# Three raw block buffers, output projections from the third head step, an earlier low half and an earlier input load

## The reference, cut to what matters

```
xn  = layernorm(x)                                  # 2048 tokens x 512
q, k, v, u = split(xn @ W_qkvu.T); q, k = silu(q), silu(k)
o   = causal linear attention with per-head decay, 16 heads of 32, a running state
A   = (u * o * rsqrt(mean(o*o) + 1e-6)) @ W_out.T
s   = xn @ w_router; idx = top 256 tokens by s      # "selected"
h   = rms_norm(xn[idx]); 16 query heads, 8 key/value heads of 128, rotary, causal softmax
x1  = xn[idx] + attention(h) @ wo
mlp = silu(rms_norm(x1) @ w_gate) * (rms_norm(x1) @ w_up) @ w_down   # inner width 2048
F   = xn, with the selected rows gated between xn[idx] and x1 + mlp
out = x + A + F
```

## Time and profile before

| | us |
|---|---|
| median of 3 runs | 521.44 (521.37 to 521.46) |
| profiled execution | 522.22 |
| its span in the profile | 520.5 |
| PE busy | 490.6 |
| DVE, ACT, POOL busy | 304.1, 230.3, 216.2 |

### The profile page before, as it was taken

The page is one execution under the profiler, slowest core; times in us unless marked ns, Lnnn a source line. Parts: engine busy times, 40 slices in busy tenths (PEclk is TensorE's granted clock), DMA queues, the critical chain, the costliest instruction groups (busy, mean ns, idle before and its releaser), DMA issues.

```text
span 520.5 us, 10501 instructions
## 1 busy us (share of the span) xinstructions
PE 490.6 (94%) x4143; PEld 448.1 (86%) x4143; DVE 304.1 (58%) x615; ACT 230.3 (44%) x404; POOL 216.2 (42%) x191
## 2 busy tenths in 40 slices
PE   6986999999999999999998988999999989999984
PEld 6976999899998998989988877898888778999773
DVE  5958468664479888662646565987675426230231
ACT  7820241212245766512232426465758765453330
POOL 3012235323023311325066666644426332778882
PEclk9997999999999999999999997999999999999999
DMA  7914242133300110002412543565556622455423
GB/s 253 372 44 128 74 122 70 55 103 102 122 23 21 45 42 21 21 21 83 161 42 83 184 161 137 169 212 172 203 173 219 215 82 82 141 163 162 161 82 40
DMA packets 32880, 62.05 MB, mean 119 GB/s; under 512 B 3440, under 2 KB 3456, under 8 KB 32704
## 3 DMA queue, kind: packets, MB, share of 16 engines
q1 hardware_dynamic: 32288, 60.08, 35.0%
q0 software_dynamic: 544, 1.31, 1.4%
HBM read 48.27 MB, written 13.12 MB: 118 GB/s over the span
## 4 chain that ended last, share of the span: by engine, by line
PE 74%; POOL 5%; issue 4%; ACT 3%; DVE 3%; DMA 3%; DVEq 0%; ACTq 0%; POOLq 0%
PE bank L1211 24%; PE bank L1165 8%; PE bank L1202 8%; PE bank L1167 8%; PE bank L1166 7%; POOL wlo L1103 4%; PE bank L1230 3%; PE bank L1274 3%; PE bank L1264 3%; PE bank L1258 3%; ACT whi L514 2%; PE bank L1421 1%; PE bank L1251 1%; DMA raw<-in_w_gate 1%; PE bank L1181 1%
## 5 line engine op out<-in xcount | busy, mean ns | idle before, releaser
L1103 POOL TENSOR_TENSOR wlo<-raw,whi 128x512 fp32r<-128x512 f32 x96 | 127.9, 1364 | 92.0 <-ACT whi L514 92.0
L1088 POOL TENSOR_TENSOR state<-kv_new,state_dec 128x512 f32<-128x512 f32 x15 | 21.8, 1452 | 126.6 <-DVE kv_new L790 126.6
L1165 PE MATMUL bank<-HTh,whi 128*128 128x256 f32 x224 | 66.2, 296 | 1.9 <-ACT whi L514 1.2
L1167 PE MATMUL bank<-HTh,wlo 128*128 128x256 f32 x224 | 64.3, 287 | 0.0
L1166 PE MATMUL bank<-HTl,whi 128*128 128x256 f32 x224 | 64.3, 287 | 0.0
L779 DVE TENSOR_TENSOR A<-bank,DEC 128x512 f32<-128x512 f32 x64 | 39.7, 682 | 31.0 <-PE bank L1230 29.9
L514 ACT ACTIVATE whi<-raw 128x2048 fp32r<-128x2048 f32 x24 | 45.8, 1910 | 22.9 <-DMA raw<-in_w_down 14.4
L1165 PEld LDWEIGHTS bank<-HTh,whi 128*128 128x128 f32 x224 | 44.0, 197 | 3.3 <-issue 2.7
L1211 PE MATMUL bank<-xTh,WKh 128*128 128x256 f32 x128 | 38.7, 302 | 6.5 <-DVE xTl L712 6.5
L1166 PEld LDWEIGHTS bank<-HTl,whi 128*128 128x128 f32 x224 | 44.0, 196 | 0.3
L1167 PEld LDWEIGHTS bank<-HTh,wlo 128*128 128x128 f32 x224 | 43.9, 196 | 0.0
(11 more groups left out here) (237 smaller groups left out, 1344.4 us busy)
## 6 DMA issues: line engine op xcount, KB each, us to landing
X<-in_x SPq DMA_DIRECT2D x16, 256.0 KB, 4.2
xn_all<-XN SPq DMA_DIRECT2D x16, 256.0 KB, 2.8
uo_all<-uo SPq DMA_DIRECT2D x16, 256.0 KB, 2.6
raw<-in_wq SPq DMA_DIRECT2D x4, 1024.0 KB, 5.3
UR<-uo_all SPq DMA_DIRECT2D x16, 256.0 KB, 4.6
XR<-in_x SPq DMA_DIRECT2D x16, 256.0 KB, 2.9
out<-XR SPq DMA_DIRECT2D x16, 256.0 KB, 2.0
raw<-in_wo SPq DMA_DIRECT2D x4, 1024.0 KB, 5.8
```

The costliest lines, as they stand in the source:

```text
L1088: Q.tensor_tensor(state[:], kv_new[:], state_dec[:], ALU.add).then_inc(state_ok, 1)
L1103: ins = Q.tensor_tensor(low[:, k, :], raw[b % 2][:, k, :], high[:, k, :].bitcast(f32), ALU.subtract)
L1165: T.matmul(dst, lh, rh, start=first, stop=False)
L1167: return T.matmul(dst, ll, rh, start=False, stop=last)
```

## The change

There are six edits. A third raw buffer is added, in room of the first stage that is free once the tokens are chosen; block 0 waits for idx_ps instead of proj_ps, and block b from 3 on for `block_lo(b-3)`. SP issues most block loads one block earlier. The high and low halves of the blocks stand earlier in ACT's and POOL's lists of slots 13 to 15; on POOL both low halves of slots 13 and 14 stand ahead of the state's sum. The output projections start in step 2 (`OUT_AT = 2`), with all their loads, halves, sums and stores. The last `rms` and `mean_square` stand in step 0, behind TensorE's unit and ACT's exponentials. In slot -1 `xt_low(3)` is first in DVE's list behind the mask, and SP issues `load_x(M + 2)` ahead of `store_xn(M)`.

```diff
-        raw = [at(f"raw{i}", 8 * i, [P, 4, DM]) for i in range(2)]
+        raw = [at(f"raw{i}", kb, [P, 4, DM]) for i, kb in enumerate((124, 0, 8))]
...
-        PT_AT, PV_AT, WO_AT = 2, 3, 4
+        PT_AT, PV_AT, WO_AT, OUT_AT = 2, 3, 4, 2
...
-            bank_jobs += [("out", h)] if h < late_outs[0] else []
+            bank_jobs += [("out", h - OUT_AT)] if 0 <= h - OUT_AT < late_outs[0] else []
...
                 k = order[b]
-                if b < 2:
+                if b == 0:
+                    sp.wait_ge(idx_ps, 1)
+                elif b < 3:
                     sp.wait_ge(proj_ps, NPROJ * (G - 1) + 2)
                 else:
-                    sp.wait_ge(fw_lo, b - 1)
-                sp.dma_start(raw[b % 2][:], source[k[0]](int(k[1]))).then_inc(raw_in[b % 2], 16)
+                    sp.wait_ge(fw_lo, b - 2)
+                sp.dma_start(raw[b % 3][:], source[k[0]](int(k[1]))).then_inc(raw_in[b % 3], 16)
...
                 for M in ln_tiles(N):
-                    store_xn(M)
                     if M + 2 < N_TILES:
                         load_x(M + 2)
+                    store_xn(M)
...
                 if N >= 1:
                     mean_square(N - 1)
+                if N == N_TILES - 3:
+                    block_hi(1)
                 if N == N_TILES - 2:
-                    block_hi(2)
-                if N == N_TILES - 1:
-                    block_hi(4)
-                    split_uo(0)
+                    block_hi(3)
...
-            mean_square(N_TILES - 1)
-            block_hi(5)
+                if N == N_TILES - 3:
+                    block_hi(2)
+                if N == N_TILES - 2:
+                    block_hi(4)
...
                     ins.then_inc(exp_ok, 1)
+                if h == 0:
+                    mean_square(N_TILES - 1)
...
                     mask(N)
+                if N == -1:
+                    xt_low(N + XT_AHEAD)
...
                 if N >= N_TILES - 3:
                     block_lo(2 * (N - (N_TILES - 3)))
+                    block_lo(2 * (N - (N_TILES - 3)) + 1)
                 if 0 <= N < N_TILES - 1:
                     new_state(N)
                 if -1 <= N < N_TILES - 1:
                     state_decayed(N + 1)
-                if N >= N_TILES - 3:
-                    block_lo(2 * (N - (N_TILES - 3)) + 1)
...
-            rms(N_TILES - 1)
...
                     unit(unit_of_step[h])
+                if h == 0:
+                    rms(N_TILES - 1)
...
-                if h < late_outs[0]:
-                    project_out(h)
+                if 0 <= h - OUT_AT < late_outs[0]:
+                    project_out(h - OUT_AT)
```

More of the change, by code:

```diff
@@ L72, in build @@
                     for part, homes in (("h", (112, 158, 96, 104)), ("l", (116, 162, 100, 108))))
-        VA = [at(f"VA{i}", kb, [P, NS, DM]) for i, kb in enumerate((92, 124))]
+        VA = [at(f"VA{i}", kb, [P, NS, DM]) for i, kb in enumerate((92, 120))]
         X = at("X", 120, [P, NX, DM])
@@ L416, in _ @@
                     load_x_again(1)
-                    load_block(4)
                 if N == N_TILES - 1:
                     load_block(5)
+                    load_block(6)
             store_uo(N_TILES - 1)
-            load_block(6)
-            load_uo(2)
+            load_block(7)
             for h in range(STEPS):
-                if h + 3 < N_TILES:
-                    load_uo(h + 3)
-                if h < late_outs[0]:
-                    store(h)
-                if h + 2 < N_TILES:
-                    load_x_again(h + 2)
+                if 2 <= h + 1 < N_TILES:
+                    load_uo(h + 1)
+                if 0 <= h - OUT_AT < late_outs[0]:
+                    store(h - OUT_AT)
+                if 2 <= h < N_TILES:
+                    load_x_again(h)
                 if h in load_at:
                     load_block(block_of[load_at[h]])
-            for b in range(block_of["U1"] + 1, len(order)):
+            for b in range(block_of["D0"] + 1, len(order)):
                 load_block(b)
-                if b == block_of["U1"] + 1:
+                if b == block_of["D0"] + 1:
                     for N in late_outs:
@@ L511, in block_hi @@
             def block_hi(b):
-                act.wait_ge(raw_in[b % 2], 16 * (b // 2 + 1))
+                act.wait_ge(raw_in[b % 3], 16 * (b // 3 + 1))
                 act.wait_ge(*last_use(b))
-                S.activation(halves(b)[0][:], raw[b % 2][:], ACT.Copy).then_inc(fw_hi, 1)
+                S.activation(halves(b)[0][:], raw[b % 3][:], ACT.Copy).then_inc(fw_hi, 1)
             def hidden_high(n):
@@ L936, in _ @@
                 in_position(N, 1)
-                if N == N_TILES - 1:
-                    uo_low(0)
-                if CH < N + XT_AHEAD < N_TILES:
+                if CH + 1 < N + XT_AHEAD < N_TILES:
                     xt_low(N + XT_AHEAD)
@@ L970, in _ @@
                     ins.then_inc(sm_ok, 1)
-                if h < late_outs[1]:
-                    uo_low(h + 1)
+                if 0 <= n + 1 < late_outs[2]:
+                    uo_low(n + 1)
                 if h < FH:
@@ L979, in _ @@
                     stage(unit_of_step[h])
-                if h < late_outs[0]:
-                    final(h)
+                if 0 <= n < late_outs[0]:
+                    final(n)
                 if 0 <= g < FH:
@@ L1102, in block_lo @@
                 for k in range(4):
-                    ins = Q.tensor_tensor(low[:, k, :], raw[b % 2][:, k, :], high[:, k, :].bitcast(f32), ALU.subtract)
+                    ins = Q.tensor_tensor(low[:, k, :], raw[b % 3][:, k, :], high[:, k, :].bitcast(f32), ALU.subtract)
                 ins.then_inc(fw_lo, 1)
```

31 lines of the change are left out of this document (15 added, 16 removed).

## The result

The changed kernel takes 508.71 us (median of four runs, 507.23 to 509.07) against 521.45 for the kernel before, which had runs of 521.37 to 523.16 beside it. The ratio is 0.9733, with a 95% interval of 0.9704 to 0.9761. The forecast was 505.6 with a range of 503.3 to 511. The profiled execution takes 508.65 with a span of 506.9, where before had 522.22 and 520.5: 13.6 us of span are gone, and 15.8 had been forecast. By the medians it is 12.7, mainly since the profiled execution of the kernel before was 0.8 above its median. So 508.71 lies inside the wide range, but above the 504 to 507.5 that went with the forecast itself.

A forecast was written before the change was run, and what follows sets the result against it. TensorE was taken as the bound, at full clock nearly everywhere, the change being worth the stops it removes: 6.1 + 4.6 + 1.6 + 3.5 = 15.8 us, from 521.44 to 505.6 us, range 503.3 to 511.

The forecast's parts named there:

- (a): Rival: the lower clock comes back behind waits in steps 2 and 3 or slot 0, costing about 3.1 us: 508.7; chance 0.18.
- (c): Rival: the early gain is halved, DVE's norms of tiles 5 to 8 slow down, keys come at 48: 508.7; chance 0.10.
- part 2: Slots 13 to 15 and steps 0 to 3: earlier block halves, later rms and moved projections gain 4.6 us, bounds 1.5 and 6.5.
- Part 1: Slot -1: xt_low(3) first and the input load ahead of the store gain 6.1 us, bounds 4.5 and 8.1.
- Part 2 up to the end of unit 8: Slots 13 to 15: stops of 1.53, 2.54 and 2.40 go; 7.6 us won, some given back later.
- Part 2 behind unit 8: Steps 0 to 3: rotations delay the first projection 1.2 us and unit 11 2.4 us, leaving 4.6 us won.
- The price of 2.9 by that rule for part 2: Steps before unit 11: if POOL slows both uo_low to 1.72 us each, the gain is 2.9 instead of 4.6.
- Part 3: Steps 13 and 14: projections moved there fill the gaps and gain 1.6 us, bounds 1.0 and 2.0.
- Part 4: The end: loads waiting for the low half three back remove stops of 1.20, 0.42 and 1.45; gain 3.5, bounds 1.5 and 3.7.
- (b): Rival: POOL and ACT, not the raw buffers, set the end's pace, which then gives 0.5: 508.6; chance 0.08.
- (d): Rival: in the middle fw_hi of blocks 3 and 5 waits for late units, stops stay, only rms moves: about 508; chance 0.08.
- (e): Rival: block loads hold up SP's one queue in steps 2 to 17, 16 us and more lost: 522 to 526; chance 0.02.

The follow-up runs named there:

- e1: Changed kernel with only xt_low(3) put back behind the norms of tiles 5 and 6, early input load kept; 510.37 us, ratio 0.9787.
- e2: Changed kernel with only SP's order put back, store_xn(M) ahead of load_x(M+2); 512.27 us, ratio 0.9811.
- e4: Changed kernel with only TensorE's last rms put back ahead of step 0, mean_square staying in step 0; 512.26 us, ratio 0.9826.
- e11: Changed kernel with POOL's second low half of a block in slots 13 to 15 put back behind the state's sum; 509.65 us, ratio 0.9773.
- e8: Changed kernel leaving out three of the four quarters of block 6's low half on POOL; 509.28 us, ratio 0.9728.
- e9: Changed kernel with DVE's rotation ahead of uo_low and the reciprocal in steps 0 to 2; 508.9 us, ratio 0.9751.
- e10: Changed kernel with the output projections starting from step 0 again (OUT_AT = 0); 506.36 us, ratio 0.9691.
- e6: Changed kernel with the output projections starting from step 1 (OUT_AT = 1); 506.57 us, ratio 0.9693.
- e3: Changed kernel with the loads of the last seven blocks waiting for the low half two blocks back, as with two buffers; 514.7 us, ratio 0.9881.
- e5: Changed kernel with DVE decaying the keys ahead of the statistics of tiles 7 and 8 in slot 0; 507.45 us, ratio 0.9703.
- e12: Changed kernel with the edits of e5, e6, e7 and e9 together, plus xt_low ahead of the norms in slot 0; 508.0 us, ratio 0.9736.
- e7: Changed kernel with 20 idle products instead of 12 at the very start; 508.29 us, ratio 0.9726.

## Why the prediction was right, and where it was off

The direction, the stages and most of the waits came as forecast. The size was 3.1 us short by the medians. That the time fell on the 508.7 of rivals (a) and (c) is luck: the first fall of the clock cost nothing, and the keys were not late. The 2.2 us that the profiles lack are 1.45 in the start and 1.9 in part 2, less 1.2 in the other stages; the other 0.9 is in the two profiled executions, of which that of the kernel before was 0.8 above its median.

**Part 1 (6.1 forecast, 6.04 measured).** Right in size and in the wait that takes its place (2.0 forecast, 1.84). e1 and e2 show that both edits are needed for it: without one or the other 2.7 and 2.9 of the 6.04 are lost.

**Part 2 up to the end of unit 8 (7.6 forecast, 7.4 measured).** 273.03 us in the profile before, 265.60 after, from the transposes of tile 4. Two of its edits are shown apart: the place of `rms` (e4: 2.6 by the end of unit 8, of which 1.3 are left at unit 11) and POOL's order (e11: 1.4). The other 3.4 us belong to the third buffer, the earlier loads and ACT's order together, and no run takes these back in the middle.

**Part 2 behind unit 8: the term that was mis-sized.** It gave the banks of the rotations of units 8 and 9 free at 3.2 and 8.6 us behind the end of unit 8. They came at 3.5 and 10.1. The largest term that was mis-sized is the last sum of unit 8's rotation, taken as 0.6 of DVE's time until the next instruction: it took 1.7, beside the low half of block 6 on POOL. The prediction's own times had them together, the sum from 319.9 and the low half from 320.1. POOL's row, and behind it the sum of unit 9's rotation, 6.6 us later with POOL idle:

```profile
315.86 5.89 POOL L1106 TENSOR_TENSOR wlo<-raw,whi 128x512 fp32r<-128x512 f32 x4
```

```profile
322.47 0.69 DVE L867 TENSOR_TENSOR QR<-rope,rope 128x512 f32<-128x512 f32 x1
```

The wait ahead of the first projection became 2.52 instead of 1.2, and unit 11 came at 16.1 us behind unit 8 instead of 14.4: 1.7 of the 1.9 us that part 2 lacks. The sum makes 1.1 of these 1.7; the rest is 0.3 on the first rotation and small terms. The prediction weighed for `uo_low` the statement of the Trainium skill ("GPSIMD Engine Reference", section "Specifications") that GpSimd and VectorE share their way into SBUF. The trace agrees with it once more (1.80 against 0.69). But it bore on the wrong instruction: `uo_low`, at 1.23, is covered by the exponentials (e8), and the sum of the rotation, which reads two SBUF operands too, is not. That the low half is the cause is borne out by e9, where the sum of unit 8's rotation starts 3.5 us ahead of that low half (317.61) and takes 0.69:

```profile
314.13 0.69 DVE L867 TENSOR_TENSOR QR<-rope,rope 128x512 f32<-128x512 f32 x1
```

That its length counts in full is seen in e4. There `rms` stands ahead of step 0, the sum starts 1.0 us behind the start of the low half (317.40) instead of with it, and takes 0.85. The low half of u*o behind it is as long as before (1.22), and the next rotation's sum starts 5.65 us behind, not 6.59. Timeline of DVE, e4:

```profile
318.39 0.85 DVE L867 TENSOR_TENSOR QR<-rope,rope 128x512 f32<-128x512 f32 x1
319.71 1.22 DVE L844 TENSOR_TENSOR uol<-UR,uoh 128x512 fp32r<-128x512 f32 x1
324.04 0.69 DVE L867 TENSOR_TENSOR QR<-rope,rope 128x512 f32<-128x512 f32 x1
```

In e4 the two banks come free 3.2 and 8.8 us behind the end of unit 8, where the prediction had 3.2 and 8.6. The price of 2.9 by that rule for part 2 was near the 2.7 measured by luck, since it came from another instruction.

**What part 2 did not see.** It took the stops ahead of the first projection and of unit 11 as the price of a full DVE, and moving the projections as free. e10 shows that the move makes these stops: with the projections in steps 0 and 1 TensorE has 2.83 us more to do in each while DVE rotates, and the stops are gone, although DVE does its `uo_low` and `final` there as well. With one projection back (e6) one stop of 2.98 is left. The early blocks and the move stood in one change, and the move took 2.7 us (3.2 less 0.5) from what the blocks gave, by the profiles, or 2.4 by the medians (506.36 against 508.71). In the prediction no part was a loss; this one is.

**Part 3 (1.6 forecast, 1.74 measured).** Right as a stage, but e10 gives the other side of the account: it has stops of together 2.17 in the last steps against 1.09, and is still ahead.

**Part 4 (3.5 forecast, 4.11 measured; bounds 1.5 to 3.7).** No stop is left there. e3 gives 4.3 for the early loads alone. The overlap between products that a stop breaks was taken too small: the stages with the stops of 1.20, 0.42 and 1.45 are 1.43, 0.66 and 1.69 shorter after, which is 0.7 of overlap and not 0.4. The last 0.3 are small gaps.

**Rivals.** (a) A fall of the clock came, at the stop of 2.52 ahead of the first projection. Its 12 matmuls took 4.42 us and not 2.83, but it cost nothing, since unit 11 waits for the rotation anyway: in e2, at full clock, the stop there is 2.18 and not 0.58. So in the changed kernel's profile (a) is right as an event and wrong in its price of 3.1. Where the fall comes one stop later, ahead of unit 11, it does cost: in e4, e5 and e8 the stretch from unit 11 to the last scores takes 83.1 to 83.2 us and not 81.7. The Trainium skill ("TensorE: Matmul & The Clock Gate", section "What's actually happening") calls the low level the default that activity releases; the profiles bear it out as far as each fall stands behind a thin stretch, but they show falls and no falls behind the same one. The 1.45 us lost in the start, for which the forecast had no term, hold a fall as well: at 0.61 from 8 to 12 us the first K product came at 12.66 instead of 11.79, and 0.6 came between there and 38.49. That stretch is 25.8 us long, and from 24.9 to 26.1 in the profiles of the twelve experiments, with 25.2 and 24.9 in e8 and e10, which have the same fall. So the fall does not explain the 0.6, and they are not shown to belong to the change. (b), (c), (d) and (e) did not happen: the end freed itself, the keys came at 45.87 and not 48, the three stops of the middle went, and no engine waits for a UR load of SP.

## What to carry to other kernels

When an engine stops for another one in some steps, ask what independent work could stand in those steps before moving any away from them: filling the stops was worth 2.4 us here by the medians, and taking the filler out looked like plain bookkeeping in the sum. Price a vector instruction by what the neighbouring engine does at its new time, and do it for every instruction on the chain and not only the one whose slow instance the trace happens to show. Moving an instruction ahead on an engine that is full in those steps (e9, e12) handed the delay to whoever waits for the one behind it.

## What the runs showed of the hardware

The same stop of TensorE is followed by a lower clock in some executions and not in others. Ahead of the transposes of tile 4 it is 1.84 to 1.91 us in nine profiles. Behind it the clock granted from 44 to 52 us stays 1.00 in five (the changed kernel, e6, e7, e9, e11) and falls in four (e3, e4, e8, e10), which makes the stretch 1.5 us longer. Windows of e9 and of e10:

```profile
48.00:52.00 4.00, 4.00 (x58) 3.68 (x58) 2.34 (x6) 1.08 (x2) 0.00 (x0) 1.00 0.91 269
```

```profile
48.00:52.00 4.00, 4.00 (x36) 3.88 (x37) 2.12 (x6) 0.60 (x1) 0.00 (x0) 0.74 0.83 241
```

With the start (0.61 to 0.64 from 8 to 12 in three of the profiles, 0.9 us) this explains how two profiles of nearly one kernel can differ by 2 us, and it is why stages are compared here from one mark to the next. In e5 and e12, where the stop is 0.35 and 0.45, the clock did not fall there. In the middle it is alike: of the changed kernel and e1, e2, e3, e5, e7, e8 and e11, all with the stop of 2.52 ahead of the first projection, the clock fell in or behind that stop in four (the changed kernel, e1, e3, e7), behind the next stop in two (e5, e8), and not at all in two (e2, e11).

The last sum of a rotation and the low half of u*o, DVE instructions on 128x512 with both operands in SBUF, took 0.68 or 0.69 us in steps 0 to 3 of every profile where no low half ran on POOL beside them, also beside POOL's `out_rms` (327.52 in the earlier trace rows). Where a low half ran beside them for more than 0.3 us they took 0.82 to 1.83.
